# Attention scores of two tiles at once on 64x64 quarters of the array, with four masked copies of q

## The reference

```python
# layer 1                                          # layer 3
q = _rope(q.reshape(B, T, 16, 16))                 attn = einsum('bhnd,bhmd->bhnm', q, k) * scale
k = _rope(k.reshape(B, T, 16, 16))                 attn = where(mask[:, None, :, :], attn, -1e9)
attn = softmax(einsum('bhqd,bhkd->bhqk', q, k)/4)  attn = softmax(attn)
out = einsum('bhqk,bhkd->bhqd', attn, v)           out = einsum('bhnm,bhmd->bhnd', attn, v)
return out @ w_ao + b_ao                           return out @ proj_w.T + proj_b
```

## Time and profile before

| | before |
|---|---|
| runs | 2108.14, 2112.38, 2114.72 us |
| profiled execution, its own time | 2109.61 us |
| its span | 2107.8 us |
| attention of layer 1, about | 363 to 645 us of the span |
| attention of layer 3, about | 1641 to 1910 us |
| granted TensorE clock, mean | 0.99 |

### The profile page before, as it was taken

The page is one execution under the profiler, slowest core; times in us unless marked ns, Lnnn a source line. Parts: engine busy times, 40 slices in busy tenths (PEclk is TensorE's granted clock), DMA queues, the critical chain, the costliest instruction groups (busy, mean ns, idle before and its releaser), DMA issues.

```text
span 2107.8 us, 44515 instructions
## 1 busy us (share of the span) xinstructions
PE 1998.3 (95%) x15460; PEld 1639.0 (78%) x15460; DVE 1307.4 (62%) x2505; ACT 1008.8 (48%) x1613; POOL 449.8 (21%) x413
## 2 busy tenths in 40 slices
PE   7999999899999999999999999998999999999998
PEld 6887887777777888877787777776888778777887
DVE  5856565777785656545545455546666777775664
ACT  3544555565653333334444444445444645554453
POOL 3632112444440101011111111112111221210000
PEclk9999999999999999999999999999999999999999
DMA  6000000111110000000000000000000000000000
GB/s 225 21 15 8 7 7 32 36 48 38 44 38 11 20 10 20 10 11 7 2 5 5 5 5 0 5 4 13 6 7 8 11 8 7 10 0 11 20 20 30
DMA packets 23525, 41.76 MB, mean 20 GB/s; under 512 B 2322, under 2 KB 13074, under 8 KB 22930
## 3 DMA queue, kind: packets, MB, share of 16 engines
q1 hardware_dynamic: 23442, 40.65, 5.8%
HBM read 28.06 MB, written 4.19 MB: 15 GB/s over the span
## 4 chain that ended last, share of the span: by engine, by line
PE 79%; DVE 11%; issue 5%; ACT 3%; POOL 1%; DVEq 0%; DMA 0%; ACTq 0%; SPq 0%; POOLq 0%
PE psum L610 20%; PE psum L612 19%; PE psum L611 19%; PE psum L705 5%; PE psum L718 3%; PE psum L652 3%; PE psum L737 2%; DVE xn L1117 2%; PE psum L803 2%; PE psum L751 2%; PE psum L694 1%; PE psum L545 1%; DVE pb L1188 1%; DVE mx L1185 1%; DVE h_lo L1138 1%
## 5 line engine op out<-in xcount | busy, mean ns | idle before, releaser
L610 PE MATMUL psum<-h_hi,w_lo 128*128 128x512 f32 x1056 | 433.1, 410 | 15.5 <-DVE h_lo L1138 8.9
L612 PE MATMUL psum<-h_hi,w_hi 128*128 128x512 f32 x1056 | 414.2, 392 | 0.0
L611 PE MATMUL psum<-h_lo,w_hi 128*128 128x512 f32 x1056 | 413.2, 391 | 0.0
L1240 DVE TENSOR_TENSOR hid_lo<-hid,hid_hi 128x512 fp32r<-128x512 f32 x256 | 193.7, 757 | 259.3 <-ACT hid_hi L991 259.3
L991 ACT ACTIVATE hid_hi<-hid 128x512 fp32r<-128x512 f32 x256 | 161.8, 632 | 219.8 <-PE psum L612 129.8
L1322 POOL TENSOR_TENSOR rstd<-ms,half_t 128x4 f32<-128x4 f32 x64 | 65.3, 1020 | 934.9 <-DVE ms L1112 481.2
L610 PEld LDWEIGHTS psum<-h_hi,w_lo 128*128 128x128 f32 x1056 | 199.2, 189 | 63.4 <-issue 13.3
L612 PEld LDWEIGHTS psum<-h_hi,w_hi 128*128 128x128 f32 x1056 | 198.8, 188 | 43.7
L1185 DVE TENSOR_REDUCE mx<-psum 128x8 f32<-128x512 f32 x192 | 132.2, 689 | 159.7 <-PE psum L694 106.2
L611 PEld LDWEIGHTS psum<-h_lo,w_hi 128*128 128x128 f32 x1056 | 199.6, 189 | 34.6
L986 ACT ACTIVATE hid<-psum,vec 128x512 f32<-128x512 f32 x192 | 131.9, 687 | 177.7 <-PE psum L612 164.0
(11 more groups left out here) (143 smaller groups left out, 3676.7 us busy)
## 6 DMA issues: line engine op xcount, KB each, us to landing
swapped<-rows SPq DMA_DIRECT2D x64, 128.0 KB, 2.0
stage<-in_w_dram SPq DMA_DIRECT2D x24, 256.0 KB, 2.7
stage<-in_w_dram SPq DMA_DIRECT2D x8, 512.0 KB, 3.6
out_dram<-xres SPq DMA_DIRECT2D x8, 512.0 KB, 2.9
xres<-in_x_dram SPq DMA_DIRECT2D x1, 3584.0 KB, 18.2
modw_mod<-in_modw_dram SPq DMA_DIRECT2D x2, 1536.0 KB, 13.6
stage<-in_w_dram SPq DMA_DIRECT2D x8, 384.0 KB, 3.3
stage<-in_w_dram SPq DMA_DIRECT2D x8, 192.0 KB, 2.4
```

The costliest lines, as they stand in the source:

```text
L610: nc.tensor.matmul(dst, s_lo, m_hi, start=start and j == 0, stop=False)
L611: nc.tensor.matmul(dst, s_hi, m_lo, start=False, stop=False)
L612: ins = nc.tensor.matmul(dst, s_hi, m_hi, start=False, stop=stop and j == len(pairs) - 1)
L1240: nc.vector.tensor_tensor(hid_lo[:, slot, :], hid32[:, slot, :], hid_hi[:, slot, :].bitcast(F32), ALU.subtract).then_inc(sem["hid"], 1)
```

## The change

For layers 1 and 3:

- A new stage `pair` does the scores of two tiles (stages k and k + 1, slots 0 and 1) on PE at once. Each product is 64 x 64 x 64: it sums over one half r of the feature rows (64 rows, four heads), takes one copy of q for one head and all 64 keys of one sequence. There are 2 tiles x 2 x 2 sequences x 2 row halves x 2 heads = 32 products for a pair. Row half r writes bank r, and each slot has 256 columns in both banks.
- q gets four masked copies instead of two (`is_head`, made by two small DVE reductions at the start), so `q_out` has four ACT instructions. The keys aren't expanded: `kx` is gone. In layer 1 the stage `k_out` goes, since DVE and POOL write `kk` directly; in layer 3 it is one instruction instead of four.
- In layer 3 the mask is four products of 256 columns for a pair, instead of two of 512.
- `pair` waits until both slots are free, and DVE starts on either tile only when both are full.
- In the table a pair stands ahead of scores 0 (k = 0), and for k = 2, 4 and 6 somewhat ahead of the scores stage that reads it. `scores` on PE is empty in layers 1 and 3.
- The clearing of `kx` on POOL goes (one memset in each of the two layers).

```diff
@@ order_of, layer 3
-        return [own("mask", 1), own("scores", 0), prev("probs_t", 7), own("q", 1), own("q_out", 1), prev("pv", 6), own("share"), nxt("load"),
+        return [own("mask", 1), own("pair", 0), own("scores", 0), prev("probs_t", 7), own("q", 1), own("q_out", 1), prev("pv", 6),
+                own("share"), nxt("load"),
...
-                own("scores", 3), own("probs_t", 2), prev("proj"), own("pv", 1), nxt("turn"),
+                own("scores", 3), own("probs_t", 2), prev("proj"), own("pv", 1), own("pair", 4), nxt("turn"),
...
@@ PE
+                elif s == "pair":
+                    for u in range(2):
+                        pe.wait_ge(sem[f"s_free{u}"], n_at(f"s_free{u}", ph, b, k // 2))
+                    pe.wait_ge(sem["q"], n_at("q", ph, b, 4 * (c + 1)))
+                    wait_alone(pe, sem["k"], n_at("k", ph, b, c + 1))
+                    if layer == 3:
+                        pe.wait_ge(sem["mask_now"], n_at("mask_now", ph, b, c + 1))
+                        for u in range(2):
+                            for r in range(2):
+                                nc.tensor.matmul(pair_scores(u)[:, r, :].rearrange("p (x w) -> p x w", w=P),
+                                                 mask_q_now[:, c, j + u, :],
+                                                 mask_k_now[:, c, j + u, :].unsqueeze(1).to_broadcast([P, 2, P]),
+                                                 start=u == 0, stop=False)
+                    for u in range(2):
+                        for x in range(2):
+                            for g in range(2):
+                                seq, o = 2 * (j + u) + g, (2 * x + g) * S
+                                for r in range(2):
+                                    rows = slice(r * S, (r + 1) * S)
+                                    for hd in range(2):
+                                        ins = nc.tensor.matmul(pair_scores(u)[hd * S:(hd + 1) * S, r, o:o + S],
+                                                               qb[rows, c, seq, 2 * x + hd, :],
+                                                               kk[rows, c, seq * S:(seq + 1) * S], start=layer == 1,
+                                                               stop=layer == 1 or u == x == g == 1)
+                        ins.then_inc(sem[f"s_full{u}"], 1)
...
-                        for g in range(2):
-                            ins = nc.tensor.matmul(dst.rearrange("p (r g k) -> p r g k", g=2, k=S)[:, :, g, :],
-                                                   qb[:, c, 2 * j + g, :, :].rearrange("p h q -> p (h q)"),
-                                                   kx[:, c, 2 * j + g, :, :], start=layer == 1, stop=layer == 1 or g == 1)
@@ ACT, q_out
-                        for hd, parity in enumerate(("even", "odd")):
-                            nc.scalar.activation(qb[:, k, :, hd, :], by_seq(q32[:, :]), ACT.Copy,
-                                                 scale=col(parity)).then_inc(sem["q"], 1)
+                        for head in range(4):
+                            nc.scalar.activation(qb[:, k, :, head, :], by_seq(q32[:, :]), ACT.Copy,
+                                                 scale=is_head[:, head:head + 1]).then_inc(sem["q"], 1)
@@ DVE, scores
+                    whole = slot if layer == 2 else 1
+                    dve.wait_ge(sem[f"s_full{whole}"], n_at(f"s_full{whole}", ph, b, k // 2 + 1))
```

More of the change, by code:

```diff
@@ L848, in stage_of @@
                     mask_table(k - 3)
-                if is_first(b) and (s, k) == ("k_out", 0):
-                    act.wait_ge(prepared, 4 if layer == 1 else 8)
+                if is_first(b) and (s, k) == ("v_out", 0):
+                    act.wait_ge(prepared, 3 if layer == 1 else 6)
+                if is_first(b) and (s, k) == ("q_out", 0):
+                    act.wait_ge(heads_told, 2)
                 if s == "q" and ph == 0 and k == 0 and is_first(b):
@@ L1336, in stage_of @@
                     pool.wait_ge(sem[f"{name}_cos"], n_at(f"{name}_cos", ph, b, k + 1))
-                    dst = (q32 if name == "q" else k32)[:, :]
-                    nc.gpsimd.tensor_tensor(dst, dst, swapped[:, which, :], ALU.add).then_inc(sem[f"{name}32"], 1)
+                    dst = q32[:, :] if name == "q" else kk[:, k, :]
+                    nc.gpsimd.tensor_tensor(dst, dst, swapped[:, which, :], ALU.add).then_inc(sem["q32" if name == "q" else "k"], 1)
                 elif s == "divide":
```

81 lines of the change are left out of this document (37 added, 44 removed).

## The result

The changed kernel takes 2175.57 us (median of 4 runs, 2173.3 to 2177.09); the kernel before took 2111.54 us beside it. The ratio is 1.0303, with a 95% interval of 1.029 to 1.0315. So it is slower, as forecast, but by 64 us and not by 20, and it lies outside the range of 2109 to 2146. The profiled execution has a span of 2174.0 us against 2107.8, 66.2 us more.

The account below looks back on a forecast made before the run. Bound: DVE, then PE in layer 1, the reverse in layer 3; both blocks end in q products, ACT copies, first scores. 2109.6 - 5.0 + 18.7 + 6.0 = 2129.3, named 2130; own range 2121 to 2138, wider 2109 to 2146.

Parts of the forecast that it names:

- layer 1, block starts: Layer 1: DVE starts 0.16 later, q chain ends 0.88 earlier; -0.72 us a block, seven times, -5.0.
- layer 3, block starts: Layer 3: +0.8 turn behind pair 4, +0.64 pair 6, +1.23 copies of q; 2.67 us a block, seven times, +18.7.
- clock, layer 3: Layer 3: lower clock behind idle times of 2.8 us, at every second of 7 block starts; +6.0 us.
- clock, layer 1: Layer 1: block start is DVE's and the clock falls there already; 0.
- the rest: Single copy of k, missing `k_out`, two memsets on ACT and POOL beside other work, reductions, last blocks: 0.
- Where the saving goes: Layer 1: of 3.04 us a block that PE saves, 0.72 arrives; PE idles about 2.8 at each block start.
- The new wait ahead of pair 2: Layer 1: PE waits for DVE to drain both slots, about 1 us; nothing lost, nothing gained.
- the order: Layer 3: pair 4 ahead of the turn delays the DVE chain to k of the next block; +0.8 us a block.
- the last term: Layer 3: start of q to next block start, 5.46 us instead of 4.23, with four copies of q; +1.23 a block.
- PE's busy time: Sign in the changed profile: it falls by 35 to 45 us while the span grows.
- The fourth: Rival: clock falls at every block start of both layers, +18 instead of +6, 2141 us; 12%.
- The first three: Rivals: PE saving comes through (2071, partly 2099 or less; 12%); DVE slack in layer 3 (2113; 14%); dearer quarters (2142; 10%).

Follow-up runs that it names:

- e9: e1 plus idle products on PE, in another bank, in the waits at block starts (layers 1 and 3) and ahead of k (layer 3): 2122.83 us, ratio 1.0007.
- e4: Changed kernel with a clearing of 128x4096 (of `qb`) put back on POOL in both places: 2180.59 us, ratio 1.0325.
- e10: Changed kernel with layer 2's loop on slot 0, later clearing, q copies in halves, turn ahead of pair 4, fewer fillers: 2107.23 us, ratio 0.9941.
- e6: e1 with the four copies of q made in two halves, each pair waiting only for its half, both layers: 2128.82 us, ratio 1.0019.
- e7: e1 with the next block's turn moved ahead of pair 4 in layer 3's order: 2131.19 us, ratio 1.0032.
- e8: Kernel before, with POOL's clearing of `kx` and vb waiting until DVE has normalised the next block: 2119.1 us, ratio 0.9955.
- e5: Kernel before, with the first instruction of layer 2's loop on PE on slot 239 of a 256-slot block: 2134.98 us, ratio 1.0054.
- e1: Changed kernel with the first instruction of layer 2's loop on PE on slot 0 of a 256-slot block: 2132.73 us, ratio 1.0087.

## Why the forecast was wrong

The cost came out more than three times as large as forecast, and most of it in places to which the prediction gave no term. The terms, by their names, in us of the span (negative is faster). "Measured" takes the block lengths of e9, where PE's waits are filled, for the block terms, and after minus e9 for the clock:

| term | forecast | measured |
|---|---|---|
| layer 1, block starts | -5.0 | -3.9 |
| layer 3, block starts | +18.7 | +21.4 |
| clock, layer 3 | +6.0 | +15.8 |
| clock, layer 1 | 0 | +3.8 |
| the two clearings, under "the rest" | 0 | -6.9 |
| code for layer 2's loop, not named | 0 | +35.6 |
| remainder | 0 | +0.3 |
| sum | +19.7 | +66.2 |

The split between blocks and clock in layer 3 is not exact: the first stretch of that row (block 0) is 33.5 us long in e9, with the clock down, and 31.95 in e4, with the clock up, so about 1.5 of the 21.4 are clock as well. The 1.0 us at layer 3's first block start is in the remainder.

- **What held.** "Where the saving goes": it goes nowhere, since PE waits for the copies of q at each block start: 2.6 to 2.8 us in layer 3, 2.8 to 3.5 in layer 1. The pair was cheaper than taken (1.09 and 1.63 us for 1.18 and 1.73). The new wait ahead of pair 2 is there (0.85 us). Layer 3's block holds to a tenth: k 26.08 us behind the block start (26.2), the order 0.75 (0.8), the full block at full clock 35.93 (36.0). Within it the last term was small by 0.2: from the start of q to the next block start it is 5.64 us (1890.62 to 1896.26), +1.41 for +1.23. Of the 2.7 us by which layer 3 was missed, 1.6 are in the last block, which I had put at nothing. The start of its first block, which was not among the seven either, came 1.0 us later (0.1 and 0.2 in e10 and e6, with the copies in halves).
- **The step that failed first: no term for the phases whose code is unchanged.** The sum has terms for block starts of layers 1 and 3 and for the clock there, and so takes for granted that all other phases keep their time. 112 more products in layer 1's loop and as many on each side of it moved layer 2's code to a place where its loop is loaded anew in each turn: 35.6 us, more than everything that was argued about. The trace of before has a hint: its instruction queue is silent for 300 us in layer 2, so the loop runs without being loaded again. That it only just does so could not be seen there.
- **The clearings at nothing.** "Beside other work: 0, as both idle for more than half of the span" asked whether POOL had time, not what it did to DVE meanwhile. DVE stood still for it. The sign was in the trace of before: the same four instructions for xn take 6.59 us in that block, 1.14 in one at the start (30.50 us) and 2.15 in the blocks of layer 1.
- **The clock term was mis-sized,** 6.0 for 19.6. Two errors. In layer 1 I put it at nothing, "the start is DVE's": but DVE now waits for the whole pair, which takes 1.98 us at the lower level, so DVE starts 0.72 us later, and where the clock fell -0.72 a block became +0.1 (34.69 us for 34.58). In layer 3 I looked only at block starts. The wait ahead of k, 0.91 us before, became 1.51, and the clock fell behind it in each of the later blocks: 2.72 us for six products that take 1.5, another 1.2. That the order put this wait up to 1.51 and so brought the fall is likely but not shown: in e7, with 1.35 us, the clock stayed up at k, yet it fell behind more block starts instead.
- **PE's busy time** was to fall by 35 to 45 us and fell by 5.6, in part because products at the lower level count as busy for longer (the first product of k 0.79 us for 0.49). As a sign it was useless.
- **The rivals.** The fourth (the clock falls at every block start) had about the right size for the clock, +18, but the wrong place for half of it. The first three are out: nothing of the PE time came through, DVE had no slack that took the layer 3 terms away, and the quarters were not dearer.

What stays open: which slots are bad. 0 is good in both kernels and 200 in the kernel before; 239 and the changed kernel's own place are bad in the changed kernel; in the kernel before, its own place stopped at two of five back edges in e8, and 239 at no more in e5. The end of a loop of 1620 instructions then lies 35 slots (from 200) or about 70 (from 239) into an eighth block. That the reach into the eighth block is what decides fits slots 0, 200 and 239 but wasn't shown by a finer sweep. The Trainium skill, page "Runtime: NRT & Kernel Launch", section "Instruction fetch mechanics", gives PE room for 2048 instructions, filled in blocks of 256, which makes eight, and says that a taken branch to a target outside the current window of two blocks forces a load before execution goes on. The stops of 2 to 4 us here look like this (10 stops, 23.8 us). But by this rule every back edge of a loop of 6.3 blocks would stop, and in the kernel before and in e1 five turns ran without one packet. The page also says that only sequential loading helps and that there is no cache; here the measurement decides against it.

## What to carry to other kernels

A change that lengthens the code in front of a loop is a change to that loop: compare the instruction queue's packets and the "issue" waits phase by phase, including the phases that were not touched, and try another place for the head of a long loop (here 1620 instructions on PE) that turns out to be loaded anew in each turn. Where the freed engine ends in a wait, price the clock behind that wait and behind each wait downstream that grows with it; filling the wait with idle products is a cheap way to measure it. Idle time of POOL is not free time: ask what DVE does at that moment. And give the kernel before the same repairs before calling the change good: here it kept the lead.

## What the hardware showed that was not expected

- A loop on PE of about 1620 instructions runs without any instruction packet in 300 us, and the same loop in another place takes 37 packets there and 35.6 us more in five turns.
- The same PE code stopped at two of five back edges in one profiled run (e8) and at none in another (the kernel before). In its unprofiled runs the kernel before took 2108.5 to 2117.3 us in the first set and 2108.6 to 2131.2 in the other two, which may be the same thing.
- A clearing of 128x4096 f32 on POOL holds up DVE's normalisation for all of its 3.53 us.
- PE starts records of 64x64x64 products on four quarters (two records a product in f32) every 17 ns at full clock (1.09 us for 64), and about every 30 ns at the lower (1.91 us).
- With PE's wait cut from 2.8 to about 2 us the granted clock fell behind more block starts, not fewer (e6, one execution); filling it with products kept it at 1.00 (e9).
